# One step's softmax division in four pieces, and the order of early transfers, row maxima and late products, in an attention and feed-forward kernel

## What is computed

```python
qkv = einsum('bsd,ed->bse', x, w_qkv) + b_qkv
scores = einsum('bhqd,bhkd->bhqk', q, k) / sqrt(32) + causal
out = einsum('bhqk,bhkd->bhqd', softmax(scores), v)
x = layernorm(x + out @ w_out.T + b_out)
hidden = relu(x @ sign(up_w).T * up_scale)
x = layernorm(x + hidden @ sign(down_w).T * down_scale * output_scale)
```

## Time and profile before

| | |
|---|---|
| median of 3 runs | 742.65 us (739.91 to 743.69) |
| profiled execution | 741.63 us, of it 739.9 us from its first to its last instruction (the span) |
| TensorE (PE) busy | 711.2 us, 96% of the span |
| VectorE (DVE) | 414.5 us, 56% |
| GpSimd (POOL) | 374.8 us, 51% |
| ScalarE (ACT) | 326.9 us, 44% |
| chain that ended last | 86% of it TensorE |

### The profile page before, as it was taken

How to read it: one execution, slowest core, us unless ns; L and a number is a source line. 1 busy time by engine, 2 the same in 40 slices (tenths; PEclk the granted TensorE clock), 3 DMA queues, 4 the chain that set the end, 5 groups by cost and what they waited for, 6 DMA issues and landing times.

```text
span 739.9 us, 11980 instructions
## 1 busy us (share of the span) xinstructions
PE 711.2 (96%) x4136; PEld 513.6 (69%) x4136; DVE 414.5 (56%) x1024; ACT 326.9 (44%) x651; POOL 374.8 (51%) x515
## 2 busy tenths in 40 slices
PE   6899999999999999999999999999899999999995
PEld 4688666665666656666544667788788787878883
DVE  4176576474765748657388541344793369324614
ACT  5211355665556656566555686522221222221213
POOL 4561458395583956839404439552452235223334
PEclk9999999999999999999999999999999999999998
DMA  7975455525646355353766564405105101000101
GB/s 240 295 231 145 130 168 147 159 88 159 181 135 160 103 147 181 114 161 101 205 183 210 159 203 136 134 20 153 30 31 154 29 1 53 5 1 0 58 1 57
DMA packets 47796, 90.03 MB, mean 122 GB/s; under 512 B 5820, under 2 KB 14780, under 8 KB 47608
## 3 DMA queue, kind: packets, MB, share of 16 engines
q1 hardware_dynamic: 38712, 84.02, 38.1%
q10 hardware_dynamic: 9024, 5.24, 2.4%
HBM read 59.38 MB, written 29.61 MB: 120 GB/s over the span
## 4 chain that ended last, share of the span: by engine, by line
PE 86%; DVE 5%; DMA 3%; ACT 2%; issue 2%; POOL 1%; SPq 0%; ACTq 0%; DVEq 0%; POOLq 0%
PE ps_proj L1127 10%; PE ps_heads L1228 9%; PE ps_proj L1280 8%; PE ps_score L1305 7%; PE ps_unit L1280 7%; PE ps_unit L1163 6%; PE ps_unit L1195 5%; PE ps_unit L1251 5%; PE ps_sum L1222 5%; PE ps_score L1195 4%; PE ps_score L1163 4%; PE ps_heads L1305 2%; PE ps_sum L1305 2%; PE ps_unit L1305 2%; PE ps_score L1147 2%
## 5 line engine op out<-in xcount | busy, mean ns | idle before, releaser
L801 POOL TENSOR_TENSOR hid_low<-hid_raw,hid_high 128x512 fp32r<-128x512 f32 (+1 forms) x80 | 91.5, 1143 | 170.5 <-DVE hid_high L1057 162.7
L858 ACT ACTIVATE probs<-ps_unit 128x512 f32<-128x512 f32 (+3 forms) x214 | 101.9, 490 | 85.4 <-PE ps_unit L1195 81.4
L764 POOL TENSOR_SCALAR_AFFINE_SELECT probs<-probs 128x128 f32<-128x128 f32 x256 | 72.8, 300 | 77.8 <-ACT probs L858 74.0
L858 ACT ACTIVATE probs<-ps_score 128x512 f32<-128x512 f32 (+3 forms) x170 | 82.4, 495 | 64.8 <-PE ps_score L1195 62.2
L969 DVE CUSTOM_DVE_ANT_0 ps_unit<-ps_unit,causal 128x128 f32<-128x128 f32 (+3 forms) x162 | 80.7, 514 | 47.0 <-PE ps_unit L1163 46.4
L1057 DVE CAST hid_high<-hid_raw 128x512 fp32r<-128x512 f32 (+1 forms) x80 | 33.0, 414 | 125.0 <-ACT hid_raw L921 124.2
L1163 PE MATMUL ps_unit<-stack 96*128 96x512 f32 (+3 forms) x242 | 82.7, 353 | 3.8 <-DMA stack<-qk_parts 1.6
L1228 PE MATMUL ps_heads<-probs,v_rows 128*32 128x512 f32 (+3 forms) x768 | 80.3, 497 | 0.0
L1195 PE MATMUL ps_unit<-stack 98*128 98x512 f32 (+2 forms) x214 | 76.4, 360 | 0.6 <-ACT probs L858 0.5
L758 POOL TENSOR_TENSOR parts<-qk_full,parts 128x512 fp32r<-128x512 f32 x32 | 41.1, 1286 | 65.2 <-ACT parts L837 65.2
L777 POOL TENSOR_TENSOR added<-added,probs 128x512 f32<-128x512 f32 x56 | 71.6, 1289 | 0.0
(11 more groups left out here) (218 smaller groups left out, 1460.5 us busy)
## 6 DMA issues: line engine op xcount, KB each, us to landing
stack<-qk_parts SPq DMA_DIRECT2D x96, 256.0 KB, 4.4
qk_parts<-parts SPq DMA_DIRECT2D x32, 512.0 KB, 2.9
v_all<-h_even ACTq DMA_DIRECT2D x16, 256.0 KB, 3.3
v_rows<-v_all SPq DMA_DIRECT2D x8, 512.0 KB, 4.1
heads_t<-heads_sb SPq DMA_DIRECT2D x16, 256.0 KB, 2.6
x_tile<-x_rows SPq DMA_DIRECT2D x16, 256.0 KB, 5.0
raw<-up_w SPq DMA_DIRECT2D x8, 512.0 KB, 3.6
raw<-down_w SPq DMA_DIRECT2D x8, 512.0 KB, 3.8
```

The lines of the kernel that those rows point to most:

```text
L764: nc.gpsimd.affine_select(out=tile, in_=tile, compare_op=ALU.is_ge, fill=0.0, base=0, pattern=[[1, P]], channel_multiplier=-1).then_inc(s_ ...
L801: nc.gpsimd.tensor_tensor(parts2[1][:, (HM * s + n) % 3, 0:tokens(s)], full[:, n % 2, 0:tokens(s)], parts2[0][:, (HM * s + n) % 3, 0:token ...
L858: nc.scalar.activation(probs[:, (NP * s + n) % RING, 0:width], bank(what, s, n)[:, off:off + width], ACT.Exp, scale=SCALE).then_inc(s_exp, 1)
```

## The change

- The start: 17 matmuls on the cleared mask, with no use of their result, run before the first projection. The casts of the x pieces 6 and 7 come after the first projection's evictions. Every second of the first four evictions writes to heads_sb in place of the one shared buffer, and waits for one low part less. The values' low weights move from GpSimd to VectorE. On SyncE the first two stacks come before the third keep and before the loads of the second batch; the bias is loaded earlier. The second batch's casts come later.
- The first score waits for the copy of value tile 14, and the first weighted sum for that of tile 15, in place of the first score for both. The first step's late row maximum and its turn come later.
- The paired steps: the first 16 maxima begin later and lie closer, and the last of four projections comes 0.7 slots earlier.
- The seventh step: the reciprocal is cut into four of 128 columns, with maxima between them; the product, and the store of these heads, follow later; 17 of its maxima are spread from slot 20.2 in place of 24.
- The feed-forward part: the second chunk's projections and turns come up to 0.7 slots earlier; the third chunk's scalings and splits come later, the last chunk's splits earlier; residuals of the first round shift by up to 0.3 slots. The last products run in pairs of tiles.

```diff
-MAXIMA = [11.5 + 0.7 * u for u in range(16)] + [23.4 + 0.73 * u for u in range(17)] + [37.5 + 0.66 * u for u in range(15)]
-LAST_MAXIMA = ([11.5 + 0.5 * u for u in range(3)] + [13.4 + 0.48 * u for u in range(13)] + [24 + 0.68 * u for u in range(17)]
+MAXIMA = [12.1 + 0.66 * u for u in range(16)] + [23.4 + 0.73 * u for u in range(17)] + [37.5 + 0.66 * u for u in range(15)]
+LAST_MAXIMA = ([12 + 0.45 * u for u in range(3)] + [13.4 + 0.48 * u for u in range(13)] + [20.2 + 0.86 * u for u in range(17)]
                + [37.5 + 0.66 * u for u in range(15)])
...
-         (2, 0, 20.5, 1.2, 34.4, 37.2, 40), (2, 1, 36.3, 0.6, 44.05, 46.8, 49.2)]
+         (2, 0, 20.5, 1.2, 34.4, 37.2, 40), (2, 1, 35.6, 0.6, 43.3, 46, 48.5)]
...
+WARM = 17
...
     for n in range(8):
-        put(-200, "x", 0, n)
+        put(-200 if n < 6 else -189, "x", 0, n)
...
-        put(-190 + 10 * k, "keep", 0, k)
-        if k > 0:
-            put(-190 + 10 * k, "stack", 0, k - 1)
-        if k == 1:
-            for c in range(DC):
-                put(-179, "wv", 0, c)
-    put(-155, "stack", 0, NB - 1)
+        put((-190, -180, -169, -160)[k], "keep", 0, k)
+        put((-171, -170, -156, -155)[k], "stack", 0, k)
+    for c in range(DC):
+        put(-179, "wv", 0, c)
     for n in range(8):
-        put(-178 if n < DC else -168, "load_x", 1, n)
-        put(-136 + 2 * n, "x", 1, n)
+        put(-158 if n < DC else -154, "load_x", 1, n)
+        put(-131 + 2 * n if n < DC else -130 + 2 * n, "x", 1, n)
     put(-153, "load_w", 1)
-    put(-119, "ones", 0)
+    put(-115, "ones", 0)
...
-    put(0.9, "row_max", 0, 1)
-    put(1.2, "shift", 0, 1)
+    put(2.4, "row_max", 0, 1)
+    put(4.4, "shift", 0, 1)
...
-            put(t + at, "copy", s, q)
-            put(t + at + (4.9 if (s, q) == AT_ONCE else 1.6), "store", s, q)
+            if (s, q) == AT_ONCE:
+                for i in range(TT):
+                    put(t + at + 1.4 * i, "divide", s, i)
+            put(t + at + (5.05 if (s, q) == AT_ONCE else 0), "copy", s, q)
+            put(t + at + (6 if (s, q) == AT_ONCE else 1.6), "store", s, q)
...
-                put(end + 1.05 + q if r else FIRST_UP + 16.2 + 2.7 * q, "ln2", i, q)
-                put(end + 1.95 + q if r else FIRST_UP + 16.7 + 2.7 * q, "out", i, q)
+                put(end + 1.05 + q if r else FIRST_UP + 15.9 + 3 * q, "ln2", i, q)
+                put(end + 1.95 + q if r else FIRST_UP + 16.4 + 3 * q, "out", i, q)
...
-                at = 2 * q if i else 2.7 * q
+                at = 2 * q if i else 2.6 * q - 0.4
                 if i:
-                    put(t + (0.7 if i == 1 else -1.4) + 0.5 * q, "scale", i + 1, q)
-                put(t + (2.2 + 0.7 * q if i else 0.3 * q - 0.8), "split", i + 1, q)
+                    put(t + (1.9 if i == 1 else -1.4) + 0.45 * q, "scale", i + 1, q)
+                put(t + ((0.3 * q - 0.8, 2.8 + 0.6 * q, 1.9 + 0.7 * q)[i]), "split", i + 1, q)
...
+        def full_sb(s, k):
+
+            return heads_sb if s == 0 and k % 2 else qk_full
...
+            sp.dma_start(bias_sb[:, :, :], b_qk).then_inc(s_bias, 16)
             sp.wait_ge(s_wd, 16)
             for n in range(4, 8):
                 load_x(0, n)
-            sp.dma_start(bias_sb[:, :, :], b_qk).then_inc(s_bias, 16)
...
-                    wait(act, s_lo, NB * s + n)
-                    nc.scalar.activation(qk_full[:, :], proj_bank(s, n)[:, :], ACT.Identity,
+                    wait(act, s_lo, NB * s + n - (s == 0))
+                    nc.scalar.activation(full_sb(s, n)[:, :], proj_bank(s, n)[:, :], ACT.Identity,
...
+                if what == "wv":
+
+                    dve.wait_ge(s_wvh, n + 1)
+                    nc.vector.tensor_tensor(wv[1][:, n, :], wv_raw[:, n, :], wv[0][:, n, :].bitcast(FP32),
+                                            ALU.subtract).then_inc(s_wvl, 1)
...
+                if what == "divide":
+
+                    if n == 0:
+                        dve.wait_ge(s_pv, NP * s + 4 * GH)
+                        dve.wait_ge(s_st[1], 16 * s)
+                    k = slice(n * P, (n + 1) * P)
+                    nc.vector.reciprocal(heads_sb[:, k], ps_sum[:, k]).then_inc(s_norm if n == TT - 1 else s_div, 1)
...
                     if (s, f) == AT_ONCE:
-                        nc.vector.reciprocal(heads_sb[:, :], ps_sum[:, :]).then_inc(s_norm, 1)
+                        dve.wait_ge(s_div, TT - 1)
                         dve.wait_ge(s_norm, 2 * s + f + 1)
...
+            pe.wait_ge(s_const, 1)
+            for m in range(WARM):
+                nc.tensor.matmul(ps_unit[1][:, 0:HALF - P], causal[:, 0:P], causal[:, 0:HALF - P], start=True, stop=True)
...
                             pe.wait_ge(s_qk, NB + 1)
-                            pe.wait_ge(s_ve, VT)
+                            pe.wait_ge(s_ve, VT - 1)
...
                         wait(pe, s_hc, 2 * s + f)
+                        if f == 0 and s == 0:
+                            pe.wait_ge(s_ve, VT)
...
-                if what == "finish":
+                if what == "finish" and n % 2 == 0:
+
                     r = len(ROUNDS) - 1
                     for m in (HM - 2, HM - 1):
                         pe.wait_ge(s_hdl, HM * r + m + 1)
-                        for part in range(2):
-                            mm = nc.tensor.matmul(ps_down[n][:, :], hid[part][:, (HM * r + m) % 3, n * P:(n + 1) * P],
-                                                  down_sb[:, down_at(m), :], start=False, stop=(m == HM - 1 and part == 1))
-                    mm.then_inc(s_dt, 1)
+                        for q in (n, n + 1):
+                            for part in range(2):
+                                mm = nc.tensor.matmul(ps_down[q][:, :], hid[part][:, (HM * r + m) % 3, q * P:(q + 1) * P],
...
+                            if m == HM - 1:
+                                mm.then_inc(s_dt, 1)
```

More of the change, by code:

```diff
@@ L738, in _ @@
                                             ALU.subtract).then_inc(s_wl, 1)
-                if what == "wv":
-                    pool.wait_ge(s_wvh, n + 1)
-                    nc.gpsimd.tensor_tensor(wv[1][:, n, :], wv_raw[:, n, :], wv[0][:, n, :].bitcast(FP32),
-                                            ALU.subtract).then_inc(s_wvl, 1)
                 if what == "ones":
@@ L1315, in _ @@
                         pe.wait_ge(s_hdl, HM * r + m + 1)
-                        for part in range(2):
-                            mm = nc.tensor.matmul(ps_down[n][:, :], hid[part][:, (HM * r + m) % 3, n * P:(n + 1) * P],
-                                                  down_sb[:, down_at(m), :], start=False, stop=(m == HM - 1 and part == 1))
-                    mm.then_inc(s_dt, 1)
+                        for q in (n, n + 1):
+                            for part in range(2):
+                                mm = nc.tensor.matmul(ps_down[q][:, :], hid[part][:, (HM * r + m) % 3, q * P:(q + 1) * P],
+                                                      down_sb[:, down_at(m), :], start=False,
+                                                      stop=(m == HM - 1 and part == 1))
+                            if m == HM - 1:
+                                mm.then_inc(s_dt, 1)
 def kernel(L0_attn_x, L0_attn_w_qkv, L0_attn_b_qkv, L0_attn_w_out, L0_attn_b_out, L0_ffn_up_weight,
```

3 lines of the change are left out of this document (2 added, 1 removed).

## The result

The changed kernel takes 754.47 us (median, 753.55 to 755.47) against 741.81 us of the kernel before in the same comparison, a ratio of 1.0171 with a 95% interval of 1.0152 to 1.0189. It is slower by 12.7 us. The forecast was 736.7 us, its range ended at 740.2, and slower had a chance of 0.04. The profiled execution took 754.11 us, its span 752.4 us, 12.5 more than that of the kernel before.

The account below looks back on a forecast made before the run. TensorE's queue of matmuls bounds the kernel, with 28.7 us idle to win plus half-rate matmuls. Terms 4.1 + 0 + 0.4 + 1.0 + 0.3 + 0.1 = 5.9 us took the median from 742.65 to 736.7 us, range 733.3 to 740.2.

Parts of the forecast that it names:

- the paired steps: Six steps with paired sums: lose or gain little, taken as 0, from -0.4 to 1.5 us for all six.
- Rival C: Closer maxima make VectorE late in every paired step, TensorE waits for banks and loses rate: 754 us, chance 0.04.
- The start: Up to the first weighted sum: four terms, 0.33 + 0.71 + 1.60 + 1.45, together 4.1 us gained.
- The first three terms: At the start: first projection 0.33 us earlier, waits for values' low weights (0.71) and first stack (1.60) gone.
- the slow pace: First projections, 2.48 and 2.11 us per four against 0.93: read as nearly half rate, which the 17 matmuls should cure.
- Rival B: At the start, transfers still land late and TensorE stands elsewhere: 2.2 us less gain, 739.0 us, chance 0.13.
- The fourth term: Before the first score: the 1.49 us wait for the last value tile's copy goes, taken as 1.45 us gained.
- The division: Seventh step, reciprocal split in four with maxima between: 0.4 us gained, bounds -0.6 and 1.3, clock fall likelier.
- The second chunk's end: Feed-forward part: waits of 1.41 and 0.51 us go, third chunk's splits come later; 1.0 us gained, between 2.1 and -0.15.
- Both signs: No wait before the third round, and a new one, about 1.2 us, before its output projection.
- 737.9: Forecast time in us if only the third chunk's splits take long (1.8 us beside GpSimd's work), chance 0.2.
- The last chunk: Its first split moves ahead of a cast into idle time, so the 0.33 us wait before its output projection goes.

Follow-up runs that it names:

- e1: The changed kernel with the paired steps' fourth projection back at slot 36.3 instead of 35.6: 743.36 us, ratio 1.0023 to the kernel before.
- e2: The kernel before with only the paired steps' fourth projection moved to slot 35.6: 753.61 us, ratio 1.0169.
- e3: The changed kernel with the third projection's eviction on ScalarE at slot 33.75 instead of 34.4, the fourth projection staying at 35.6: 748.28 us, ratio 1.0092.
- e7: The kernel before with the start's changes alone, including the first score's shorter wait and the first step's later maximum and turn: 740.03 us, ratio 0.9968.
- e12: e9 with six buffers instead of three for value tiles on their way out: 735.36 us, ratio 0.9922 to the kernel before.
- e4: The kernel before with the seventh step's part alone: division in four pieces, later product and store, new maxima slots: 744.64 us, ratio 1.0048.
- e10: e9 with the division in four pieces and later product and store, but that step's maxima at their old slots: 736.17 us, ratio 0.9924.
- e14: e13 with six maxima between the division's pieces, ahead of the weighted sum, the other eleven at their old slots: 734.83 us, ratio 0.9899.
- e8: e1 with one undivided reciprocal, the seventh step's second 17 maxima from slot 26.5, and later residuals ahead of the third chunk: 739.35 us, ratio 0.9960.
- e6: e1 with the division undone: one reciprocal and the seventh step's maxima at their old slots: 742.02 us, ratio 0.9991 to the kernel before.
- e9: The changed kernel with the fourth projection's slot, the third chunk's scalings and splits, and the division with its maxima undone: 737.32 us, ratio 0.9934.
- e5: e1 with the third chunk's scalings and splits back at their old slots: 739.48 us, ratio 0.9961 to the kernel before.
- e11: e10 with six maxima between the division's pieces and eleven spread wider behind the weighted sum: 738.94 us, ratio 0.9961 to the kernel before.
- e13: e9 with both the four pieces of e10 and the six buffers of e12: 734.60 us, ratio 0.9901 to the kernel before.

## Why the prediction was wrong

**The step that failed: the paired steps at 0, from -0.4 to 1.5.** Of the edits there the prediction weighed the maxima alone. The fourth projection's earlier slot was in the list of changes and was given neither a cost nor a cover, so the term stood at nothing without a reason. To ask which work it crosses on TensorE would have shown the 16 products of slot 36 between 35.6 and 36.3, and the trace before has the eviction that they covered: two of ScalarE's instructions that end 1.2 us behind the point at which TensorE reaches the weighted sum (298.31 to 299.52). With six steps this is 7.2 us of idle time; to it come some 0.4 us of slower products round each wait (45.62 us busy in the step from 267.03, against 45.21 in the same step before) and, in the profile after, a stretch at the low clock (the step from 170.65 to 219.62 has a mean clock of 0.97). e1 and e2 put the whole at 11 to 12 us. A new idle entry in the paired steps was one of the signs that the prediction named for being wrong, and it came.

**Rival C** forecast 754 us and was right in nothing else. What it priced, maxima late in each paired step, is not there: in the five steps to the sixth sum TensorE waits 1.9 us for maxima in the kernel before and 1.9 us in the kernel after, the one entry of 0.38 us in each step. That its time came was luck. A time that agrees does not show a mechanism; this row and e1 to e3 tell the two apart.

**The start: 4.1 forecast, 2.4 measured (e7).** The first three terms came. The first product of a maximum starts 3.35 us earlier (32.04 against 35.39 in the earlier trace rows), with no wait for the first stack or for the values' low weights, where 0.33 + 0.71 + 1.60 = 2.64 had been summed. In part this is because an idle entry is less than what the wait costs from start to start: in the kernel before, three products and the wait behind them take 1.58 us at the entry of 0.71 (22.58 to 24.16) and 2.47 us at that of 1.60 (32.92 to 35.39), and three such products without a wait take 0.70. The first projection ends 0.32 us earlier, as bounded, but the slow pace was read wrongly: at a granted clock of 1.00 its first four products still take 2.24 us (6.66 to 8.90), since they wait for casts.

Then 1.8 us went back before the first product with the second batch's x. The prediction looked for a late transfer among stacks and loads of x. The loads took up to 10.9 us to land instead of 7.3, but no engine is shown waiting for one. What was late were the stores of value tiles, which now share the time from 23 to 40 us with the loads and the second pair of stacks. The three buffers were not free, so VectorE waited 8.1 us in four places instead of 3.5 in one, and TensorE's maxima with it. Rival B was thus right in kind and wrong in the transfer.

The fourth term gave half. The wait of 1.49 before the first score went, but in ScalarE's order the store of value tile 15 stands ahead of the first exponential, so that ScalarE now waits for the copy in TensorE's place, and TensorE soon waits for banks that ScalarE has not read (profile after):

```profile
82.78 0.37 ACTq L820 DMA_DIRECT2D v_all<-h_even  x1
83.27 1.08 ACT L859 ACTIVATE probs<-ps_score 128x512 f32<-128x512 f32 x2 [12.93 <-PE ps_unit L1213]
...
83.92 0.45 PE L1213 MATMUL ps_score<-stack 98*128 98x384 f32 x1 [0.69 <-ACT probs L859]
84.99 0.27 PE L1192 MATMUL ps_unit<-ident,row_max 128*16 128x128 f32 x1 [0.39 <-ACT probs L859]
```

From the start of the last value tile to the first weighted sum it is 10.68 us (77.81 to 88.49), against 11.38 before: 0.7 us gained in place of 1.45. With six buffers (e12) the first weighted sum starts 4.1 us ahead of the kernel before. That this is the predicted sum is luck: 0.7 too little in the first three terms and 0.7 too much in the fourth.

**The division: 0.4 gained forecast, 2.4 lost in the trace and 3.0 in e4.** The queue was worked out rightly: four pieces, the product and seven maxima were to take 8.3 us, and took 8.4 (386.84 to 395.20), with pieces of 0.95 us. Mis-sized was the clock. The bounds took it to fall as before, 1.6 us with the weighted sum and its sums. It fell 1.9 us before the weighted sum (the clock of 0.81 in 392 to 396 is 1.5 us at half rate) and stayed low twice as long, 3.4 us lost in place of 1.7. With the 1.2 GHz already ahead of it, the weighted sum came 2.9 us later in its step, not 2.1. Of the 2.4 us lost, 1.7 are thus the clock; the other 0.7 is near the 0.4 that the prediction's own terms give without it (2.1 - 0.94 - 0.8). e10 and e14 show that neither the pieces nor the maxima between them did it. What is left is the number of maxima ahead of the weighted sum, and the profiles bear it out: from the sum of added pieces of the sixth step to that weighted sum it is 30.6 us with three of them (e8), 31.7 to 32.4 with six (before, e6, e7, e9 to e14) and 34.6 to 35.2 with ten (after, e1, e3, e4, e5).
The Trainium skill (TensorE: Matmul & The Clock Gate, A second HAM failure mode: psum-queue depth-cycling) tells of a TensorE that idles briefly and often while it goes round its banks and changes between full and half rate. The rows of this case agree more with this than with the long gaps of the section that the prediction cited: the gaps around the fall at 394.5 were 0.38, 0.67 and 0.46 us.

**The second chunk's end: 1.0 gained forecast, 0.5 lost.** Both signs were foreseen. The turn's wait of 1.41 and the wait of 0.51 in the earlier trace rows went (1.59 us to the third round's first up product, and no entry at the first down product), and the foreseen wait ahead of the third chunk's output projection came. It is 2.9 us, above the long end of 2.4. The bounds of 2.1 and -0.15 do not follow from the terms beside them, either: 1.41 + 0.51 less a wait of 0.2 or 2.4 makes 1.7 and -0.5, and -0.5 is what came. The loss of 0.9 that the prediction gives for it does not agree with its own 737.9, which is 1.2 above the forecast. The term that was mis-sized is VectorE's queue there (start, us, operation):

```profile
545.52 0.68 DVE L1025 TENSOR_TENSOR t_even_low<-heads_raw,t_even_high 128x512 fp32r<-128x512 f32 x1
550.02 1.78 DVE L1025 TENSOR_TENSOR t_even_low<-heads_raw,t_even_high 128x512 fp32r<-128x512 f32 x1
552.06 0.68 DVE L1025 TENSOR_TENSOR t_even_low<-heads_raw,t_even_high 128x512 fp32r<-128x512 f32 x1
552.66 1.76 DVE L1087 TENSOR_TENSOR z_sb<-z_sb,h_even 128x512 f32<-128x512 f32 x1
555.28 0.81 DVE L1025 TENSOR_TENSOR t_even_low<-heads_raw,t_even_high 128x512 fp32r<-128x512 f32 x1
```

The splits together stayed inside the bounds; the residual in front of the last one took 1.76 us, beside GpSimd's subtraction from 552.22 to 553.88, where 0.68 had been assumed. The Trainium skill (SBUF — State Buffer, Who interferes with whom) gives its exclusion, against a GpSimd instruction that reads SBUF, for a VectorE instruction with two inputs in SBUF. The residual's 1.76 against 0.68 agrees; the prediction had applied it to the splits alone. The later scalings and splits were not needed: e5 has neither wait.

**The last chunk** gave 0.32 us where 0.33 was forecast, and the end 0.08 where 0.1 was.

**Sum.** The span was to fall by 5.9 us and rose by 12.5, 18.4 us apart: 12.2 in the six paired steps (7.2 of it idle time that the trace before could have given), 2.8 in the seventh, 1.9 in the start, 1.5 at the second chunk's end. Without the moved projection the change would have measured 743.4 us (e1), 0.2% over the kernel before; without the division and the third chunk's shifts as well, 737.3 (e9), which is the forecast within 0.6 us. That too is luck, since e9 has neither the division nor the third chunk's shifts: its start gave 2.1 us in place of 4.1, its second chunk's end 2.6 in place of 1.0.

## What to carry to other kernels

A slot that moves by a little is an edit of the order: list which instructions it crosses on its engine, and ask of each whether it was the cover of somebody's eviction. Where several matmuls share one bank, the work between the last write of the one and the first write of the next is part of the schedule, and it must be as long as the reading of the bank. When transfers are moved forward, look at who holds a buffer until a transfer lands, not only at who waits for its data.

## What the runs showed of the hardware

A fall of the clock to 1.2 GHz in the seventh step cost the same amount in many profiles: 1.7 us (before, e6 to e9, e14), or twice that, 3.4 us, in one stretch (after, e3, e5) or in two (e1, e4, e11); there was none in e10, e12 and e13. The cost is read as the length of a stretch times one less the granted clock. And it is not fixed by the code: e9 and e12 have the same instructions in that step and nearly the same gaps ahead of the weighted sum (0.69 and 0.48 us in e9, 0.71 and 0.47 in e12). In e9 the clock fell and the step took 54.54 us, in e12 it did not and the step took 53.31. Two of the four runs of e13 had a mean clock of 0.996 (733.9 and 734.0 us), two of 0.994 (735.2 and 736.0 us); where in the latter the clock was low, no profile shows. What decides was not found. A difference of under 2 us between two kernels of this kind can therefore be one such stretch.
